# Four graph layers: the MPNN pass over blocks of node tiles, with the edges' own terms scattered into slots

## What is computed

```python
x = _layernorm(x + GCN(x, edge_index, edge_weight))     # sum over edges of norm * (x @ W)[src]
x = _layernorm(x + GGNN(x, edge_index, edge_type))      # twice: agg = sum of trans[type, src]; GRU(agg, h)
x = _layernorm(x + GAT(x, edge_index))                  # 8 heads, softmax over the edges of one src
x = _layernorm(x + MPNN(x, edge_index, edge_attr))
```

```python
g_edges = jnp.broadcast_to(global_state[None, :], (num_edges, GLOB_D))
msg_in = jnp.concatenate([node_state[src], edge_state, g_edges], axis=-1)
messages = _linear(jax.nn.relu(_linear(msg_in, Wm1, bm1)), Wm2, bm2)
aggregated = jax.ops.segment_sum(messages, dst, num_segments=num_nodes)
aggregated = aggregated / jnp.maximum(degree, 1.0)[:, None]
upd_in = jnp.concatenate([node_state, aggregated, g_nodes], axis=-1)
delta = _linear(jax.nn.relu(_linear(upd_in, Wu1, bu1)), Wu2, bu2)
h = node_state + delta      # and the MPNN's own layernorm
```

## Time and profile before

| | us |
|---|---|
| median of the unprofiled runs (3) | 12518.77 |
| lowest, highest | 12474.06, 12527.3 |
| span of the profiled execution | 10787.3 |

### The profile page before, as it was taken

One profiled execution on the slowest core, in us unless ns is written; L12 is line 12 of the kernel. 1 busy time (PEld: TensorE's weight loads), 2 busy tenths in 40 slices (PEclk: granted clock), 3 DMA queues, 4 the chain that ended last, 5 costly groups with the idle time before them and its releaser, 6 DMA issues. The chain is left out here.

```text
span 10787.3 us, 166167 instructions
## 1 busy us (share of the span) xinstructions
...
## 2 busy tenths in 40 slices
...
GB/s 46 0 0 0 0 46 83 83 83 118 79 66 66 53 66 66 66 72 53 52 52 52 52 52 52 163 292 190 112 93 92 63 54 79 79 80 79 73 79 73
DMA packets 322858, 798.38 MB, mean 74 GB/s; under 512 B 157570, under 2 KB 196012, under 8 KB 303436
## 3 DMA queue, kind: packets, MB, share of 16 engines
...
...
## 5 line engine op out<-in xcount | busy, mean ns | idle before, releaser
L984 POOL DMA_INDIRECT ggnn_edges_G<-trans_d,ggnn_edges_rid x3136 | 2975.5, 949 | 1199.3 <-issue 955.1
L1097 PE MATMUL ggnn_edges_PS<-ggnn_edges_OH,ggnn_edges_G 128*128 128x128 f32 x6272 | 1176.8, 373 | 2317.1 <-DMA ggnn_edges_G<-trans_d,ggnn_edges_rid 2207.2
L1097 PEld LDWEIGHTS ggnn_edges_PS<-ggnn_edges_OH,ggnn_edges_G 128*128 128x128 f32 x6272 | 1136.7, 285 | 2361.7 <-issue 2360.2
L984 POOL DMA_INDIRECT mpnn_edges_G<-msg_d,mpnn_edges_rid x1568 | 1499.8, 956 | 659.5 <-issue 473.0
L1053 DVE TENSOR_TENSOR acc<-acc,ggnn_edges_PS 128x128 f32 x224 | 64.6, 288 | 2510.7 <-PE ggnn_edges_PS L1097 2510.7
L1081 PE MATMUL mpnn_edges_PS<-wt_late,mpnn_edges_at 128*128 128x256 f32 x1568 | 545.3, 522 | 682.1 <-DVE mpnn_edges_G L1040 339.9
L620 ACT ACTIVATE prep_OJF<-prep_OJ,prep_fld 128x98 bf16<-128x98 bf16 x3136 | 848.9, 362 | 555.0 <-DVE prep_OJ L676 555.0
L1081 PEld LDWEIGHTS mpnn_edges_PS<-wt_late,mpnn_edges_at 128*128 128x128 f32 x1568 | 414.8, 272 | 794.1 <-DVE mpnn_edges_G L1040 361.1
L826 PE MATMUL prep_PS<-prep_OJF,prep_OHr 128*128 128x490 bf16 x1582 | 580.7, 549 | 211.5 <-DVE prep_OHr L705 211.5
L1040 DVE TENSOR_TENSOR mpnn_edges_G<-mpnn_edges_G,mpnn_edges_PS 128x1792 f32<-128x1792 f32 x112 | 226.3, 2020 | 878.9 <-DMA mpnn_edges_G<-msg_d,mpnn_edges_rid 702.0
L1018 DVE SCALAR_TENSOR_TENSOR ggnn_edges_OH<-dstI,ggnn_edges_itm,ggnn_edges_PS 128x896 f32<-128x896 f32 x448 | 491.6, 1144 | 228.7 <-issue 164.1
...
## 6 DMA issues: line engine op xcount, KB each, us to landing
ba_rows<-slot_d SPq DMA_DIRECT2D x49, 3136.0 KB, 11.4
...
ggnn_edges_G<-trans_d,ggnn_edges_rid POOLq DMA_INDIRECT x3136, 2.5
mpnn_edges_at<-in_edge_attr SPq DMA_DIRECT2D x112, 448.0 KB, 3.6
trans_d<-gcn_edges_tb ACTq DMA_DIRECT2D x49, 512.0 KB, 2.7
trans_d<-ggnn_edges_tb ACTq DMA_DIRECT2D x49, 512.0 KB, 3.0
mpnn_edges_G<-msg_d,mpnn_edges_rid POOLq DMA_INDIRECT x1568, 2.5
```

The lines of the kernel that those rows point to most:

```text
L984: pool.indirect_dma_start(G[:, s, c, :], None, table, bass.IndirectOffsetOnAxis(ap=rid[:, s, c:c + 1].bitcast(U32), axis=0)).then_inc(gath ...
L1097: mm = pe.matmul(wp[s % 2], G[:, s, c, :], OH[:, s % 2, c, :], start=c == 0, stop=c == GC - 1)
```

## The change

1. **prep** clears a new array in DRAM, slots_d: 49 x 128 x 49 slots of 128 floats (157 MB), in 112 pieces, one behind each load of an item by SP. At its end DVE computes for each edge the number of its slot (tile of the target, rank, tile of the source; edges beyond rank 127 get a row behind the slots), kept in place_d.
2. **GGNN passes**: before the items of each of the 14 chunks, PE multiplies 8 groups of edges with W_M1E (7 matmuls a group), ACT copies the products from PSUM and stores them into rows_d. 112 groups in all.
3. **max** loads place_d over dstI.
4. **ba, heads, gat_edges** get a program for GpSimd, `place_rows`: 34, 56 and 22 groups. For a group: one load of its rows (128 x 7168 B) into SBUF, one copy of its 14 x 128 slot numbers, 14 indirect DMAs, each of which scatters 128 rows of 512 B into slots_d. In gat_edges they come behind the 28 gathers. A stage ends when all are placed.
5. **msgs**, a third use of `block_pass`, takes the place of the MPNN pass over items: it fetches rows of the message table as heads does, adds the own terms loaded from slots_d (ab, four buffers, one load a unit by SP), applies the relu on ACT, and adds up two units behind the fetch (lag = 2).
6. **mpnn_edges** keeps the overflow edges (turns_o, 28 gathers, 2 slots) and the seven chunk ends. Since it is `late = False`, each chunk's end is completed before the next chunk begins.
7. heads uses HB for its rows of slots, and so SP's first load there waits until the splits have read it; KEY0 is freed after gcn; edge_attr has two groups more.

The core of the diff:

```diff
+NSLOT = NT * P * NT
+AG = NG // (2 * NCH)
+HQ = [4, GC // 2 - 4]
+PL_BA, PL_HEADS, PL_GAT = 34, 56, 22
...
@@ prep @@
+                    sp.wait_ge(blanked, 1)
+                    with sp.Fori(0, NG // SL) as i:
                         for s in range(SL):
-                            sp.wait_ge(done, i * SL + s + 1)
-                            sp.dma_start(itm[:, s, :], items_d[ds(i * SL + s, 1), :].to_broadcast([P, 4])
-                                         ).then_inc(item_ready[s], 16)
+                            next_item(i, s)
+                            sp.dma_start(blank_d[ds(i * SL + s, 1)].rearrange("g p a n -> (g p) a n"), rows(blank[:], ZN)
+                                         ).then_inc(wiped, 16)
...
+                    own.step(V.tensor_single_scalar(tileI, dstI[:], 7, op=ALU.arith_shift_right))
+                    own.step(V.scalar_tensor_tensor(out=KEY0[:], in0=RK[:], scalar=float(NT), in1=KEY0[:],
+                                                    op0=ALU.mult, op1=ALU.add))
+                    own.step(V.scalar_tensor_tensor(out=KEY0[:], in0=tileI, scalar=float((P - 1) * NT), in1=KEY0[:],
+                                                    op0=ALU.mult, op1=ALU.add))
+                    own.step(V.tensor_scalar(tileF, RK[:], float(2 * P), float(2 * NSLOT), ALU.is_ge, ALU.mult))
+                    own.step(V.tensor_tensor(out=KEY0[:], in0=KEY0[:], in1=tileF, op=ALU.add))
+                    own.step(V.scalar_tensor_tensor(out=slotI.rearrange("p (k n) -> p k n", n=NWASTE),
...
@@ new: placing @@
+                def load(g, b):
+                    pool.dma_start(buf[:, b], rows_d[ds(g, 1)].rearrange("g p f -> (g p) f")).then_inc(read[b], 16)
+
+                def scatter(b, c):
+                    pool.indirect_dma_start(slots_d, bass.IndirectOffsetOnAxis(ap=sid[:, b, c:c + 1].bitcast(U32), axis=0),
+                                            buf[:, b, c * D:(c + 1) * D], None).then_inc(placed[b], 16)
+
+                def group(i, b, fresh=False, end=False):
+                    g = i * 2 + (g0 + b)
+                    nc.gpsimd.tensor_copy(sid[:, b], dstI[:, ds(g * GC, GC)]).then_inc(numbers, 1)
+                    pool.wait_ge(read[b], i * 16 + 16)
+                    pool.wait_ge(numbers, i * 2 + (b + 1))
+                    passed(pool, tick)
+                    for c in range(GC // 2):
+                        scatter(b, c)
+                    if not fresh:
+                        pool.wait_ge(placed[1 - b], i * (16 * GC) + b * 16 * GC)
+                        passed(pool, tick)
+                    if not end:
+                        load(g + 1, 1 - b)
+                    for c in range(GC // 2, GC):
+                        scatter(b, c)
...
@@ new: attr_rows @@
+                def tensor(self, pe, c):
+                    if table:
+                        table.emptied(pe, c)
+                    for k in range(AG):
+                        pe.wait_ge(at_in[k % 2], c * (AG // 2 * 16) + (k // 2 + 1) * 16)
+                        for h in range(2):
+                            pe.wait_ge(free, c * (2 * AG) + (2 * k + h + 1))
+                            for q in range(4 * h, 4 * h + HQ[h]):
+                                mm = pe.matmul(ep[:, q, :], at_[:, k % 2, q, :], W(W_M1E, 2), start=True, stop=True)
+                            mm.then_inc(ready, 1)
...
+                            act.copy(held[:, h, 0:n], ep[:, 4 * h:4 * h + HQ[h]].rearrange("p q n -> p (q n)")).then_inc(free, 1)
+                            act.wait_ge(free, c * (2 * AG) + (2 * k + h + 3))
+                            act.dma_start(rows_d[ds(g, 1), :, 8 * h * D:8 * h * D + n].rearrange("g p f -> (g p) f"),
+                                          held[:, h, 0:n]).then_inc(stored[h], 16)
+                        self.load(act, g + 2, k % 2)
...
@@ block_pass @@
+                        def load_attr(n, ip):
+                            for u in range(U):
+                                v = ip * U + u
+                                sp.wait_ge(weighed, n * W2 + (v + W2 - 3))
+                                sp.dma_start(ab[:, v % 4, 0:HU[u], :].rearrange("p b f -> p (b f)"),
...
+                            elif msgs:
+                                if nb > 12:
+                                    V.tensor_tensor(out=msg[:, par, 12], in0=odd, in1=ab[:, v % 4, 12, :], op=ALU.add)
+                                V.tensor_tensor(out=msg[:, par, 0:12], in0=gp[par], in1=ab[:, v % 4, 0:12, :],
+                                                op=ALU.add).then_inc(weighed, 1)
...
+                        def relu(n, v):
+                            act.wait_ge(weighed, n * W2 + v + W2 + 1)
+                            act.activation(msg[:, v % 2, 0:HU[v % U]], msg[:, v % 2, 0:HU[v % U]], ACT.Relu).then_inc(relued, 1)
...
+                        lag = 2 if msgs else 1
...
@@ the calls @@
-            aggregate(f"ggnn{l}_edges", trans_d[l].rearrange("n (t f) -> (n t) f", t=T), row_d, stage, sl=2 * SL)
+            aggregate(f"ggnn{l}_edges", trans_d[l].rearrange("n (t f) -> (n t) f", t=T), row_d, stage, sl=2 * SL, g0=l * (NG // 2))
...
-        block_attention("ba")
+        block_attention("ba", places=(0, PL_BA))
...
-        block_pass("heads", recd=recD[:])
-        aggregate("gat_edges", heads_d, src_d, gat_end, rest="factors", sl=FS)
+        block_pass("heads", recd=recD[:], places=(PL_BA, PL_HEADS))
+        aggregate("gat_edges", heads_d, src_d, gat_end, rest="factors", sl=FS, places=(PL_BA + PL_HEADS, PL_GAT))
+        block_pass("msgs", recd=recD[:])
         gat.close()
-        aggregate("mpnn_edges", msg_d, src_d, mpnn_end, attr=True, sl=SL)
+        aggregate("mpnn_edges", msg_d, src_d, mpnn_end, rest="bare", attr=True, sl=FS)
```

272 lines of the change are left out of this document (221 added, 51 removed).

## The result

| | before | after |
|---|---|---|
| median of the unprofiled runs, us | 12512.08 | 12814.46 |
| lowest, highest | 12474.06, 12527.3 | 12791.36, 12834.4 |
| span of the profiled execution | 10787.3 | 12819.1 |

The ratio after to before is 1.0239, 95% interval 1.0222 to 1.0255: the change makes the kernel about 2.4% slower on the chip of this comparison. The forecast was 12585, range 12400 to 12770: the direction was right, the time lies above the range. A run more than 1.5% above the fastest of the same kernel is not compared; there is one, in e5.

The account below looks back on a forecast made before the run. GpSimd's indirect DMAs, 1.25 us a row, were taken to bound the GGNN and MPNN passes, PE heads. -730 + 5 + 12 + 779 = +66 us on the 12518.77 median gave 12585, range 12400 to 12770.

Parts of the forecast that it names:

- the clock of this sum: Whole kernel: sum made in span time, added unchanged to the 12518.77 us median; 1731 us between them in no row.
- MPNN, -730: MPNN pass: 2052 us replaced by msgs (985), mpnn_edges (334) and a stage boundary (3), 1322 us together.
- Products, +5: GGNN passes: edges' own terms, 40 to 48 us a chunk on PE, hidden behind GpSimd's gathers; +5 us.
- GpSimd must run ahead: it has 8 slots: GGNN chunk borders: 8 slots of 14 gathers give 140 us, enough for chunk end plus products, 92 us.
- Prep, +12: Prep: 112 blank pieces hidden behind item loads; DVE passes at the tail about 8.5 us, plus store and memset.
- Scatters, +779: ba, heads, gat_edges: scatters delayed beside DVE, the remainder exposed after DVE finishes: +199, +305, +275 us.
- The load of a group: GpSimd's load of 128x7168 B before each group's scatters: 0.94 to 2.5 us, 0.94 taken; the upper value adds 74 us.
- A: ba, heads, gat_edges: DVE does not hold the scatters up; +401 in place of +779, 12207 us; chance 0.14.
- B: msgs: bound by its loads, slower, at 206 GB/s; +172 us, 12757 us; chance 0.12.
- C: GGNN passes: attribute phase does not fit, GpSimd waits at each of 14 chunks; +112, 12697 us; chance 0.12.
- D: Scatter stages: every scatter beside DVE held 3.58 us; net +815, 13334 us; chance 0.04.
- the sum's own range: Whole sum: -40 (cheaper overflow, handing over, scatters) to +90 (loads, slower msgs unit), giving 12540 to 12675 us.

Follow-up runs that it names:

- e5: Kernel after with the 112 blank pieces written in gcn instead of prep: 12906.75 to 13202.42 us against 12575.9 for before, slower kind of chip.
- e2: Kernel after without the scatters and without the GGNN passes' products with edge attributes: 10112.99 us, faster kind of chip.
- e9: Kernel after with the blank pieces written in gcn instead of prep, faster kind of chip: 10841.3 us, ratio 1.0053 to before.
- e1: Kernel after without the scatters, their loads and index copies (slots stay blank): 10113.19 us, faster kind of chip.
- e3: Kernel after, unedited, on the faster kind of chip: 10893.27 us against 10799.93 for before, ratio 1.0087.
- e8: Kernel after with heads' one-hot of the targets cut to one block, faster kind of chip: 10709.25 us against 10785.44 for before.

## Why the prediction was wrong, point by point

- **The step that failed is "the clock of this sum".** It took the 1731 us as lying outside the span and constant, and so added terms read on one kind of chip to a median from the other. In its place: the time is the span plus 1.8 us, and the difference (1765.5 us between the two spans of before) lies in the two passes with GpSimd's gathers, in which PE creeps: 1051 in GGNN and 710 in MPNN. On kind 2 the terms themselves change: GGNN +412 for +5, ba +643 for +199, MPNN -1424 for -730, +266 for +66 in all. That the total is off by no more than that is the cancelling of large misses. The working mentions that a proportional 16% would make +66 into +77; neither reading was right, because the steps sit only where GpSimd issues, which is just what the change moves about. An overlap of scatters with attention is worth its forecast only where PE can work beside GpSimd.
- **MPNN, -730:** -732 on kind 1 (msgs 977 where 985 was forecast, what follows 344 to the end of the span where 337; row `9568.00:10546.00`). Right in mechanism and size, with two small misses that cancel. On kind 2 -1424.
- **Products, +5:** +6 on kind 1, which is chip against chip; e2 shows them free (1 us). On kind 2 the GGNN passes take 412 us more. The step "GpSimd must run ahead: it has 8 slots" took them for empty; on kind 2 PE lags behind, they are full at twelve of the fourteen phases, and the products lie bare (468 us of phases, 412 lost; argued, not tested on kind 2).
- **Prep, +12:** +49. The tail's passes over 128x1568 were sized well (about 9 us), but "hidden" for the 112 pieces was wrong: a loop turn of four items lost about 1.5 us on DVE and an item 0.4. I took the transfer's 5.1 us against an item's 12 for cover, and didn't ask what else in the loop the pieces delay. e9 confirms the place: prep is 49 us shorter when the pieces leave. Which wait they lengthen stays open.
- **Scatters, +779:** 778.6 by e1 and e3. By parts, with the tails behind DVE's last instruction: ba 347 of 476 in cover (330 forecast), tail 178 us (199); heads 567 of 784 (561), tail 299 (305); gat_edges 105 of 308 (106), tail 279 (275). 1.37 us for one in the tails (1.364). The tails are 23 us shorter than forecast, and DVE's own work ends some 20 us later than before the change (3 in ba, 16 in heads, 2 in gat_edges), which the forecast did not count; the two misses cancel. On kind 2 this step fails in ba alone: next to nothing of DVE's work lay beside the scatters there.
- **The load of a group** as a GpSimd DMA holds it 0.57 to 0.59 us (bounds 0.94 to 2.5, 0.94 taken): below the lower bound, 112 x 0.36 = 40 us too much, hidden in the sum by slightly longer scatters (0.962 for a gather's 0.944) and by the copy of the slot numbers (0.21 us, and 0.81 more to the scatter behind it, where 0.4 was counted).
- **Rivals.** A is out by e8 and by the 2.41 us row; B by msgs at 978 us on both kinds with a DMA share of 0.67; C by e2 on kind 1, though on kind 2 GpSimd does stand still in twelve phases; D by 1.72 us a scatter in heads, the longest there being 2.58. B's time, 12757, comes nearest to the result by chance, C's 12697 next. C's reason (groups of over 12 us) isn't the one seen where GpSimd stands still: a group takes 5 us there. Only in the first phase of each pass on kind 2 does a group take 21 us, and there GpSimd goes on.
- **The range** was made from costs inside the sum. On kind 1 the sum's own range was -40 to +90, measured +93 by the timed runs: missed by prep's 37 us. The doubt that mattered, which machine the number stands for, had no width at all.
